# Transposing an attention step's probabilities: one DMA of 36 blocks in place of four of 2 to 16

## The chip, the cores and the metric

The kernel runs on one core of a Trainium2 chip, written directly against the engines: each of TensorE (PE), VectorE (DVE), ScalarE (ACT), GpSimd (POOL) and SyncE (SP) has a hand-written program, and semaphores order them. The metric is the time of one execution on the device in microseconds, the median of the runs of a kernel.

## The reference, cut to what matters

Two transformer blocks over 1024 tokens of width 256. The first attention and feed-forward are short here. What the change touches is the second attention: 32 heads of 64, 8 key/value heads (four query heads share one), rotary embedding, a causal mask, softmax, and the product with the values.

```python
x = x + _L0_attn_ref(_layernorm(x), Wq, Wk, Wv, Wo)
x = x + _L0_ffn_ref(_layernorm(x), w_gate_up, w_down)
x = x + _L1_attn_ref(_layernorm(x), wq, wk, wv, wo)
x = x + _L1_ffn_ref(_layernorm(x), w_fc, w_proj)

# _L1_attn_ref
xq = xq * cos + _rotate_half(xq) * sin
xk = xk * cos + _rotate_half(xk) * sin
scores = einsum('bqhd,bkhd->bhqk', xq, xk) * scale
scores = where(causal, scores, -inf)
probs = softmax(scores, axis=-1)
out = einsum('bhqk,bkhd->bqhd', probs, xv)
return out.reshape(...) @ wo
```

## The kernel before, in words

**Steps.** The second attention runs in 64 steps G (`STEPS`), eight for each of the 8 key/value groups. A step holds two heads and two query tiles of 128 rows, in two parts: with r = G % 4, part 0 has a query tile of 5 + r key blocks, part 1 one of 4 - r key blocks (`blocks`). With two heads that is 10, 12, 14 or 16 blocks of 128x128 in part 0 and 8, 6, 4 or 2 in part 1, 18 in every step.

**One step on its engines.** TensorE computes the scores of a part (L1330, and the mask by L1335). VectorE takes the row maxima (L964). ScalarE takes four exponentials (`exp_unit`, L658, two for each part) into `probs` in float32. The probabilities are then split in two float16 numbers: ScalarE casts them to the high part (`p_high`, L668), and GpSimd subtracts that from `probs` for the low part (`p_low`, L492). SP issues DMA transposes of the high and low parts (L371 and L377), since the product with the values needs the keys on the partitions. Three steps later (`PV_LAG = 3`) TensorE multiplies them with the values (`pv`): for each of the 18 blocks, high part times high values (L1353) and low values (L1357), then low part times high values (L1353). VectorE divides by the sum (L971, L973).

**Buffers.** `probs` and the two parts (`p16_hi`, `p16_lo`) have two buffers each, the transposed ones (`pT_hi`, `pT_lo`) three. So the exponentials of step G wait for the low parts of G-2, the high cast of part 0 of step G waits for the landing of both high transposes of G-2, the low part of G for both low ones of G-2, and the transposes of G for the `pv` of G-3.

**Order on each engine.** Each engine takes its instructions in order. ScalarE in step G: the high cast of part 1 of G-1, exponential 0, exponential 1, the high cast of part 0, exponentials 2 and 3, with copies for other work between them. TensorE's scores of a part wait for the exponentials of the same part of the step before (`exp_done`). GpSimd in step G: the rotary additions that fall due (L477, L480; eight of them in the first four steps of a group), low part 0, low part 1; in the sixth step of a group the low part of the next weights (`split_wkq_low`, L465) stands between the two, in the third the low part of the output weights (`split_wo_low`, L470), and the latter also in the last step of all. SP in step G: weight loads in two steps of a group, then the transposes high 0, high 1, low 0, low 1, each with a wait for its own part and a semaphore of its own.

**Other work.** `JOBS` lays the projections, transposes and output products of neighbouring groups between the scores and `pv` on TensorE. When the last `pv` is done, the output product, and after it the last feed-forward, follow.

**Names in the rows.** A program's tiles are shown with buffer numbers left out: `p_hi` and `p_lo` are the float16 parts, `pT_hi` and `pT_lo` their transposes.

Of the kernel before, what the change touches and what calls it, by code (L numbers as in the profile page):

```python
# [16 lines left out]
F32R = mybir.dt.float32r  # L17
F16 = mybir.dt.float16
# [5 lines left out]
P = 128  # L24
# [7 lines left out]
def transformer_program(nc, x_in, wq_a, wk_a, wv_a, wo_a, w_gate_up, w_down,  # L32
# [3 lines left out]
    KC = C // P  # L36
# [10 lines left out]
    def sb(name, kb, shape, dt):  # L47

        return nc.alloc_sbuf_tensor_at(name, [P] + shape, dt, offset=base + int(kb * 1024))
# [50 lines left out]
    v_lo = sb("v_lo", 88.25, [NT, NG * HEAD], F16)  # L100

    KQ = 5 * HEAD
    wkq_hi = sb("wkq_hi", 64.5, [KC, KQ], F32R)
    wkq_lo = sb("wkq_lo", 67, [KC, KQ], F32R)
    wo_nat = sb("wo_nat", 69.5, [2, C], F32)
    wo_hi = sb("wo_hi", 71.5, [2, C], F32R)
    wo_lo = sb("wo_lo", 73.5, [2, C], F32R)
# [6 lines left out]
    qT = [sb(f"qT{p}", 154 + 8 * p, [T], F32) for p in range(2)]  # L114

    probs = [sb(f"probs{b}", 42 + 9 * b, [18 * P], F32) for b in range(2)]
    p16_hi = [sb(f"p16_hi{b}", 186 + 9 * b, [18 * P], F16) for b in range(2)]
    p16_lo = [sb(f"p16_lo{b}", 190.5 + 9 * b, [18 * P], F16) for b in range(2)]
    pT_hi = [sb(f"pT_hi{b}", kb, [18, P], F16) for b, kb in enumerate((26, 30.5, 104.5))]
    pT_lo = [sb(f"pT_lo{b}", kb, [18, P], F16) for b, kb in enumerate((60, 128, 132.5))]  # L120
    o32 = [sb(f"o32{b}", kb, [4, HEAD], F32) for b, kb in enumerate((109.5, 110.5, 78, 79))]
    oT_hi = sb("oT_hi", 170, [2, T], F32R)
    oT_lo = sb("oT_lo", 178, [2, T], F32R)
# [38 lines left out]
    with ExitStack() as ctx:  # L162
        PS = ctx.enter_context(nc.psum_tensor("PS", [P, 8 * BANK], F32))

        def bank(b, n=1):
            return PS[:, b * BANK:(b + n) * BANK]
# [5 lines left out]
        def sem(name):  # L172
            return ctx.enter_context(nc.semaphore(name))
# [53 lines left out]

        scores_done, nmax_done, exp_done = sem("scores_done"), sem("nmax_done"), sem("exp_done")
        p_hi_done, p_lo_done = sem("p_hi_done"), sem("p_lo_done")
        pT_hi_landed = [[sem(f"pT_hi_landed{part}{b}") for b in range(3)] for part in range(2)]  # L230
        pT_lo_landed = [[sem(f"pT_lo_landed{part}{b}") for b in range(3)] for part in range(2)]
        pv_done, recip_done, norm_done = sem("pv_done"), sem("recip_done"), sem("norm_done")
        oT_done, oT_hi_done, oT_lo_done = sem("oT_done"), sem("oT_hi_done"), sem("oT_lo_done")
        wo_done = sem("wo_done")
# [26 lines left out]
        def of_step(G):  # L261
            g, n = G // 8, G % 8
            return g, n, n // 4, n % 4

        def blocks(G, part):
            r = G % 4
            return 4 - r if part else 5 + r
# [4 lines left out]
        def part_cols(G, part):  # L272
            n = 2 * blocks(G, 0)
            return slice(n, 18) if part else slice(0, n)
# [56 lines left out]
        def _(sp):  # L331
# [16 lines left out]
            def load_wkq(g):  # L348
                sp.dma_start(wkq_nat[:, :, 0:HEAD], rows(wk_b)[:, :, g * HEAD:(g + 1) * HEAD]).then_inc(wkq_landed, 16)
                sp.dma_start(wkq_nat[:, :, HEAD:KQ],  # L350
                             rows(wq_b)[:, :, 4 * g * HEAD:4 * (g + 1) * HEAD]).then_inc(wkq_landed, 16)
# [13 lines left out]
            load_wkq(1)  # L365
            sp.wait_ge(ternT_landed, 32)

            def transpose_hi(G, part):
                sp.wait_ge(p_hi_done, 2 * G + part + 1)
                sl = part_cols(G, part)  # L370
                sp.dma_start(pT_hi[G % 3][:, sl, :], p16_hi[G % 2][:, sl.start * P:sl.stop * P], transpose=True)\  # L371
                  .then_inc(pT_hi_landed[part][G % 3], 16)

            def transpose_lo(G, part):
                sp.wait_ge(p_lo_done, 2 * G + part + 1)
                sl = part_cols(G, part)
                sp.dma_start(pT_lo[G % 3][:, sl, :], p16_lo[G % 2][:, sl.start * P:sl.stop * P], transpose=True)\  # L377
                  .then_inc(pT_lo_landed[part][G % 3], 16)

            for G in range(STEPS):  # L380
                g, n, p, r = of_step(G)
                if n == 0 and g + 2 < NG:
                    sp.wait_ge(wkq_split, g + 2)
                    load_wkq(g + 2)
                if n == 4:
                    if g:
                        sp.wait_ge(wo_split, g)
                    load_wo(g)
                if G >= 3:
                    sp.wait_ge(pv_done, G - 2)  # L390
                transpose_hi(G, 0)
                transpose_hi(G, 1)
                transpose_lo(G, 0)
                transpose_lo(G, 1)

            for t in range(NT):
                sp.wait_ge(result_done, t + 1)
# [5 lines left out]
        def _(pool):  # L403
# [80 lines left out]
            def p_low(G, part):  # L484

                sl = part_cols(G, part)
                cols = slice(sl.start * P, sl.stop * P)
                pool.wait_ge(p_hi_done, 2 * G + part + 1)
                if G >= 2 and part == 0:
                    for landed in pT_lo_landed:  # L490
                        pool.wait_ge(landed[(G - 2) % 3], 16 * ((G - 2) // 3 + 1))
                nc.gpsimd.tensor_tensor(p16_lo[G % 2][:, cols], probs[G % 2][:, cols], p16_hi[G % 2][:, cols],  # L492
                                        ALU.subtract).then_inc(p_lo_done, 1)

            pool.wait_ge(gate_up_done, 2 * NF)
# [8 lines left out]
            for G in range(STEPS):  # L504
                g, n, p, r = of_step(G)
# [36 lines left out]
        def _(act):  # L542
# [118 lines left out]
            def p_high(G, part):  # L661
                sl = part_cols(G, part)
                cols = slice(sl.start * P, sl.stop * P)
                act.wait_ge(exp_done, 4 * G + 2 * part + 2)
                if G >= 2 and part == 0:
                    for landed in pT_hi_landed:
                        act.wait_ge(landed[(G - 2) % 3], 16 * ((G - 2) // 3 + 1))
                nc.scalar.copy(p16_hi[G % 2][:, cols], probs[G % 2][:, cols]).then_inc(p_hi_done, 1)  # L668

            split_wkq_high(0)  # L670
            for c in range(KC):
# [13 lines left out]
            for G in range(STEPS):  # L685
                g, n, p, r = of_step(G)
# [414 lines left out]
        def _(pe):  # L1101
# [238 lines left out]
            def pv(G, b):  # L1340

                g, buf, turn = G // 8, G % 3, G // 3 + 1
                o = bank(b)
                first = True
                for pT, landed in ((pT_hi, pT_hi_landed), (pT_lo, pT_lo_landed)):
                    for part in range(2):
                        pe.wait_ge(landed[part][buf], 16 * turn)
                        n, c = blocks(G, part), part_cols(G, part).start
                        for a in range(2):
                            u = (2 * part + a) * (HEAD + 1)  # L1350
                            for j in range(n):
                                p_block = pT[buf][:, c + a * n + j, :]
                                last = nc.tensor.matmul(o[:, u:u + HEAD + 1], p_block, v_hi[:, j, g, :], start=first,  # L1353
                                                        stop=False, skip_group_check=True)
                                first = False
                                if pT is pT_hi:
                                    nc.tensor.matmul(o[:, u:u + HEAD], p_block, v_lo[:, j, g * HEAD:(g + 1) * HEAD],  # L1357
                                                     start=False, stop=False, skip_group_check=True)
                last.then_inc(pv_done, 1)
# [153 lines left out]
```

## Time and profile before

| | us |
|---|---|
| median of 3 runs | 715.66 |
| lowest and highest | 710.64, 716.04 |
| the profiled execution | 710.78 |
| its span, first to last instruction | 709.0 |
| mean granted TensorE clock | 0.961 of full speed |

| engine | busy us | share |
|---|---|---|
| TensorE | 608.9 | 86% |
| GpSimd | 457.5 | 65% |
| ScalarE | 443.8 | 63% |
| VectorE | 436.8 | 62% |
| DMA queue of SP and its transposes | | 70.7% of 16 engines |

The page is one execution. Busy time is summed by engine; the slices show how it lies in time; the chain of what ended last and the waits show who was waited for. The attention in question runs from about 160 to 644 us. Most of its DMA traffic are the transposes: 36 blocks of 32 KB a step.

### The profile page before, as it was taken

Reading aid. Unit: us, or ns where it says so; the run is one execution under the profiler, and the core shown is the slowest. Engines: PE = TensorE matmul, PEld = TensorE weight load, DVE = VectorE, ACT = ScalarE, POOL = GpSimd, SP = SyncE. Lnnn points to the kernel's source line nnn. Section 1 sums busy time; section 2 is a strip of 40 time slices with the busy share of each in tenths; the row PEclk is TensorE's granted clock in tenths of the full one; section 3 lists DMA queues with packets and bytes.
Section 4 is the critical chain, followed back from the end, with each engine's and each line's share of the span. In section 5 each row is a group of like instructions: output and inputs, shape, how many; then the busy total and the mean of one; then the engine's idle time right before and its main releaser. Section 6 shows DMA issues by size and latency. Waiting matters only on the chain.

```text
span 709.0 us, 16178 instructions
## 1 busy us (share of the span) xinstructions
PE 608.9 (86%) x6750; PEld 478.5 (67%) x6750; DVE 436.8 (62%) x714; ACT 443.8 (63%) x599; POOL 457.5 (65%) x404
## 2 busy tenths in 40 slices
PE   4979988999879898987988889898798986975796
PEld 2767777986657776775776677677577664864375
DVE  5384377466657555755765675576576554555796
ACT  2223401148787677777867866877786788560695
POOL 6032155247979966977988698599689577562221
PEclk9998999999999999999999999999999999899699
DMA  9050003106999999999999999998999999991001
GB/s 296 1 178 1 1 0 67 31 0 120 153 173 171 176 169 159 177 160 182 164 168 179 165 176 160 176 178 158 186 160 159 173 159 176 182 147 35 1 23 37
DMA packets 321288, 91.76 MB, mean 129 GB/s; under 512 B 310080, under 2 KB 320320, under 8 KB 321216
## 3 DMA queue, kind: packets, MB, share of 16 engines
q1 hardware_dynamic: 320128, 89.69, 70.7%
q8 instruction: 53, 0.87, 0.5%
q10 hardware_dynamic: 1088, 1.05, 0.4%
q14 instruction: 19, 0.16, 0.1%
HBM read 13.11 MB, written 1.05 MB: 20 GB/s over the span
## 4 chain that ended last, share of the span: by engine, by line
PE 54%; DVE 14%; POOL 11%; ACT 10%; issue 5%; DMA 4%; SPq 1%; POOLq 0%; ACTq 0%; DVEq 0%
PE PS L1105 27%; PE PS L1330 13%; DVE small L964 7%; POOL p_lo L492 7%; PE PS L1353 5%; ACT probs L658 4%; PE PS L1270 3%; DMA pT_lo<-p_lo 3%; ACT p_hi L668 3%; PE PS L1357 2%; ACT oT_hi L639 2%; DVE oT_lo L979 1%; PE PS L1335 1%; POOL roped L480 1%; DMA pT_hi<-p_hi 1%
## 5 line engine op out<-in xcount | busy, mean ns | idle before, releaser
L492 POOL TENSOR_TENSOR p_lo<-probs,p_hi 128x1280 f16<-128x1280 f32 (+7 forms) x128 | 302.8, 2383 | 84.1 <-ACT p_hi L668 62.9
L658 ACT ACTIVATE probs<-PS,small 128x640 f32<-128x640 f32 (+7 forms) x256 | 183.6, 741 | 101.4 <-DVE small L964 101.4
L964 DVE TENSOR_REDUCE small<-PS 128x2 f32<-128x1280 f32 (+7 forms) x128 | 173.4, 1355 | 72.4 <-PE PS L1335 72.0
L1330 PE MATMUL PS<-kT,qT 64*128 64x512 f32 (+3 forms) x768 | 160.3, 522 | 23.7 <-ACT probs L658 22.5
L668 ACT CAST p_hi<-probs 128x1280 f16<-128x1280 f32 (+7 forms) x128 | 147.7, 1154 | 12.6 <-DMA pT_hi<-p_hi 9.2
L1330 PEld LDWEIGHTS PS<-kT,qT 64*128 64x128 f32 x768 | 65.0, 187 | 68.5 <-issue 57.1
L1353 PE MATMUL PS<-v_hi,pT_hi 128*128 128x65 f16 x1152 | 83.7, 199 | 4.1 <-DVE oT_lo L979 2.5
L1357 PE MATMUL PS<-v_lo,pT_hi 128*128 128x64 f16 x1152 | 83.2, 199 | 0.0
L1353 PEld LDWEIGHTS PS<-v_hi,pT_hi 128*128 128x128 f16 x1152 | 77.3, 102 | 8.0 <-DVE oT_lo L979 2.9
L1357 PEld LDWEIGHTS PS<-v_lo,pT_hi 128*128 128x128 f16 x1152 | 77.1, 101 | 0.4
L1105 PE MATMUL PS<-wo_hi,oT_hi 128*128 128x256 f32 x128 | 39.5, 308 | 17.1 <-DVE oT_lo L979 14.9
L979 DVE TENSOR_TENSOR oT_lo<-PS,oT_hi 128x512 fp32r<-128x512 f32 x32 | 22.1, 692 | 49.7 <-ACT oT_hi L639 49.7
L1335 PEld LDWEIGHTS PS<-mask_rows,pick_rows 64*128 64x128 bf16 x512 | 26.9, 96 | 33.9 <-issue 25.2
L1353 PE MATMUL PS<-v_hi,pT_lo 128*128 128x65 f16 x1152 | 46.6, 195 | 0.8 <-DMA pT_lo<-p_lo 0.8
L451 POOL TENSOR_TENSOR hT_lo<-h,hT_hi 128x512 fp32r<-128x512 f32 x16 | 23.6, 1479 | 36.5 <-DVE hT_hi L845 29.2
L480 POOL TENSOR_TENSOR roped<-t_cos,t_sin 128x256 f32<-128x256 f32 x64 | 47.1, 735 | 0.0
L1105 PE MATMUL PS<-wkq_hi,xnT_hi 128*128 128x320 f32 x128 | 44.8, 350 | 1.7 <-ACT qT L635 0.9
L440 POOL TENSOR_SCALAR moments<-moments 128x1 f32<-128x1 f32 x32 | 7.6, 236 | 58.4 <-DVE moments L756 57.8
L477 POOL TENSOR_TENSOR roped<-t_cos,t_sin 128x128 f32<-128x128 f32 x64 | 29.5, 461 | 19.8 <-DVE t_sin L924 19.8
L920 DVE TENSOR_TENSOR t_cos<-PS,cs 128x320 f32<-128x320 f32 x64 | 31.1, 486 | 17.0 <-POOL roped L480 9.2
L1353 PEld LDWEIGHTS PS<-v_hi,pT_lo 128*128 128x128 f16 x1152 | 40.4, 99 | 1.1 <-DMA pT_lo<-p_lo 1.1
L1270 PE MATMUL PS<-identf,roped 128*128 128x128 f32 x192 | 31.9, 298 | 9.8 <-DVE oT_lo L979 9.8
(184 smaller groups left out, 1248.2 us busy)
## 6 DMA issues: line engine op xcount, KB each, us to landing
wgu_nat<-L_ffn_w_gate_up SPq DMA_DIRECT2D x2, 1024.0 KB, 11.1
wkq_nat<-L_attn_wq SPq DMA_DIRECT2D x8, 256.0 KB, 3.5
pT_hi<-p_hi SPq DMA_TRANSPOSE x128, 4.0
pT_lo<-p_lo SPq DMA_TRANSPOSE x128, 4.1
wo_nat<-L_attn_wo SPq DMA_DIRECT2D x8, 256.0 KB, 3.4
x<-L_attn_x SPq DMA_DIRECT2D x4, 256.0 KB, 5.6
wdn_nat<-L_ffn_w_down SPq DMA_DIRECT2D x1, 1024.0 KB, 12.9
wfc_nat<-L_ffn_w_fc SPq DMA_DIRECT2D x1, 1024.0 KB, 5.8
```

Source lines behind the costliest of these rows:

```text
L480: nc.gpsimd.tensor_tensor(roped[:, t, P:3 * P], t_cos[b][:, 1:5, :].rearrange("p h d -> p (h d)"), t_sin[b][:, 1:5, :].rearrange("p h d -> ...
L492: nc.gpsimd.tensor_tensor(p16_lo[G % 2][:, cols], probs[G % 2][:, cols], p16_hi[G % 2][:, cols], ALU.subtract).then_inc(p_lo_done, 1)
L658: nc.scalar.activation(probs[G % 2][:, start:start + w], PS[:, src:src + w], ACT.Exp, bias=nmax[:, 4 * (G % 2) + u:4 * (G % 2) + u + 1]).t ...
L668: nc.scalar.copy(p16_hi[G % 2][:, cols], probs[G % 2][:, cols]).then_inc(p_hi_done, 1)
L920: nc.vector.tensor_tensor(t_cos[d][:], raw, cs[:, t, 0:HEAD].unsqueeze(1).broadcast_to(heads), ALU.mult)
L964: nc.vector.tensor_reduce(nmax[:, first:first + 2], both_heads(part)[:, :, 0:blocks(G, part) * P], AX.X, ALU.max, negate=True).then_inc(nm ...
L1105: last = nc.tensor.matmul(dst, lhsT, rhs, start=n == 0, stop=n == len(pairs) - 1)
L1270: last = nc.tensor.transpose(bank(b)[:, q * P:(q + 1) * P], roped[:, 4 * half + q, first:first + P], identf[:])
L1330: last = nc.tensor.matmul(dst[a], qT[p][rows_of[a], q_cols], kT[g % 2][rows_of[a], cols], start=True, stop=c0 + w < width, skip_group_chec ...
L1335: last = nc.tensor.matmul(dst[a][:, w - P:w], picked[rows_of[a], :], masked[rows_of[a], :], start=False, stop=m == 1, skip_group_check=True)
L1353: last = nc.tensor.matmul(o[:, u:u + HEAD + 1], p_block, v_hi[:, j, g, :], start=first, stop=False, skip_group_check=True)
L1357: nc.tensor.matmul(o[:, u:u + HEAD], p_block, v_lo[:, j, g * HEAD:(g + 1) * HEAD], start=False, stop=False, skip_group_check=True)
```

## The change

The high and low parts of a step share one buffer (`p16`, 2 x 18 blocks a partition), and so do their transposes (`pT`). SP issues one DMA transpose of all 36 blocks, when both low parts of the step are done, with one semaphore. The high cast and the low part of step G wait for the landing of this one transfer of step G-2. `pv` waits once, at its start. Two weight tiles (`wkq_hi`, `wkq_lo`) move to another place in memory to make room. The products and their order are as before.

```diff
-    wkq_hi = sb("wkq_hi", 64.5, [KC, KQ], F32R)
-    wkq_lo = sb("wkq_lo", 67, [KC, KQ], F32R)
+    wkq_hi = sb("wkq_hi", 104.5, [KC, KQ], F32R)
+    wkq_lo = sb("wkq_lo", 107, [KC, KQ], F32R)
...
-    p16_hi = [sb(f"p16_hi{b}", 186 + 9 * b, [18 * P], F16) for b in range(2)]
-    p16_lo = [sb(f"p16_lo{b}", 190.5 + 9 * b, [18 * P], F16) for b in range(2)]
-    pT_hi = [sb(f"pT_hi{b}", kb, [18, P], F16) for b, kb in enumerate((26, 30.5, 104.5))]
-    pT_lo = [sb(f"pT_lo{b}", kb, [18, P], F16) for b, kb in enumerate((60, 128, 132.5))]
+    p16 = [sb(f"p16_{b}", 186 + 9 * b, [2, 18 * P], F16) for b in range(2)]
+    pT = [sb(f"pT{b}", kb, [2, 18, P], F16) for b, kb in enumerate((26, 128, 60))]
...
-            def transpose_hi(G, part):
-                sp.wait_ge(p_hi_done, 2 * G + part + 1)
-                sl = part_cols(G, part)
-                sp.dma_start(pT_hi[G % 3][:, sl, :], p16_hi[G % 2][:, sl.start * P:sl.stop * P], transpose=True)\
-                  .then_inc(pT_hi_landed[part][G % 3], 16)
-
-            def transpose_lo(G, part):
-                sp.wait_ge(p_lo_done, 2 * G + part + 1)
-                sl = part_cols(G, part)
-                sp.dma_start(pT_lo[G % 3][:, sl, :], p16_lo[G % 2][:, sl.start * P:sl.stop * P], transpose=True)\
-                  .then_inc(pT_lo_landed[part][G % 3], 16)
+            def transpose_both(G):
+                sp.wait_ge(p_lo_done, 2 * G + 2)
+                sp.dma_start(pT[G % 3][:].rearrange("p s n q -> p (s n) q"),
+                             p16[G % 2][:].rearrange("p s n -> p (s n)"), transpose=True)\
+                  .then_inc(pT_landed[G % 3], 16)
...
-                transpose_hi(G, 0)
-                transpose_hi(G, 1)
-                transpose_lo(G, 0)
-                transpose_lo(G, 1)
+                transpose_both(G)
...
                 if G >= 2 and part == 0:
-                    for landed in pT_lo_landed:
-                        pool.wait_ge(landed[(G - 2) % 3], 16 * ((G - 2) // 3 + 1))
+                    pool.wait_ge(pT_landed[(G - 2) % 3], 16 * ((G - 2) // 3 + 1))
...
                 if G >= 2 and part == 0:
-                    for landed in pT_hi_landed:
-                        act.wait_ge(landed[(G - 2) % 3], 16 * ((G - 2) // 3 + 1))
-                nc.scalar.copy(p16_hi[G % 2][:, cols], probs[G % 2][:, cols]).then_inc(p_hi_done, 1)
+                    act.wait_ge(pT_landed[(G - 2) % 3], 16 * ((G - 2) // 3 + 1))
+                nc.scalar.copy(p16[G % 2][:, 0, cols], probs[G % 2][:, cols]).then_inc(p_hi_done, 1)
...
-                for pT, landed in ((pT_hi, pT_hi_landed), (pT_lo, pT_lo_landed)):
+                pe.wait_ge(pT_landed[buf], 16 * turn)
+                for s in range(2):
                     for part in range(2):
-                        pe.wait_ge(landed[part][buf], 16 * turn)
```

## Rows read from the trace of the kernel before

**Rows 1.** The page's slices, 40 of the span: share of DMA, in tenths

```profile
DMA  9050003106999999999999999998999999991001
```

**Rows 2.** Busy time by stretch: PE, PEld, DVE, ACT, POOL; clock; DMA share; GB/s

```profile
345.50:406.50 61.00, 55.38 (x730) 43.00 (x732) 38.30 (x58) 45.77 (x61) 49.31 (x36) 0.97 0.99 170
```

**Rows 3.** Waits from 200 to 620 us: total us, times, longest

```profile
POOL p_lo L492 <- DMA pT_lo<-p_lo: 21.0, 11, 3.5
...
PE PS L1330 <- ACT probs L658: 20.3, 10, 2.7
...
ACT p_hi L668 <- DMA pT_hi<-p_hi: 9.2, 8, 2.0
```

**Rows 4.** SP in order of time, steps 24 and 25: start, duration, line

```profile
347.00 3.07 SPq L371 DMA_TRANSPOSE pT_hi<-p_hi  x2
350.12 2.92 SPq L377 DMA_TRANSPOSE pT_lo<-p_lo  x2
353.14 3.21 SPq L371 DMA_TRANSPOSE pT_hi<-p_hi  x2
```

**Rows 5.** Tile pT_lo, step 24's two transposes, issued at 350.1 and 351.6 us

```profile
DMA to landing us min/median/max: 3.4/3.5/3.5
```

**Rows 6.** GpSimd in order of time: steps 0, 8, 24, 26, 28, 29, 32, 36, 56, 63

```profile
165.87 4.73 POOL L492 TENSOR_TENSOR p_lo<-probs,p_hi 128x1280 f16<-128x1280 f32 x2
...
218.85 4.72 POOL L492 TENSOR_TENSOR p_lo<-probs,p_hi 128x1280 f16<-128x1280 f32 x2
...
340.80 4.73 POOL L492 TENSOR_TENSOR p_lo<-probs,p_hi 128x1280 f16<-128x1280 f32 x2
...
360.90 1.15 POOL L492 TENSOR_TENSOR p_lo<-probs,p_hi 128x512 f16<-128x512 f32 x1
...
370.89 4.73 POOL L492 TENSOR_TENSOR p_lo<-probs,p_hi 128x1280 f16<-128x1280 f32 x2 [1.94 <-DMA pT_lo<-p_lo]
...
381.16 1.53 POOL L465 TENSOR_TENSOR wkq_lo<-wkq_nat,wkq_hi 128x640 fp32r<-128x640 f32 x1
...
401.75 4.73 POOL L492 TENSOR_TENSOR p_lo<-probs,p_hi 128x1280 f16<-128x1280 f32 x2
...
432.40 2.15 POOL L492 TENSOR_TENSOR p_lo<-probs,p_hi 128x1024 f16<-128x1024 f32 x1 [0.32 <-ACT p_hi L668]
...
583.22 2.13 POOL L492 TENSOR_TENSOR p_lo<-probs,p_hi 128x1024 f16<-128x1024 f32 x1 [0.85 <-ACT p_hi L668]
...
638.59 0.67 POOL L492 TENSOR_TENSOR p_lo<-probs,p_hi 128x256 f16<-128x256 f32 x1
```

**Rows 7.** To landing: all pT_hi; fcT, 16 blocks; pT_hi at 396.5 us, 16 blocks

```profile
DMA to landing us min/median/max: 2.3/4.0/6.1
...
fcT<-tern SPq DMA_TRANSPOSE x1, 4.5
...
DMA to landing us min/median/max: 5.6/5.6/5.6
```

**Rows 8.** ScalarE's high cast by shape, 330 to 390 us: busy, mean ns

```profile
L668 ACT CAST p_hi<-probs 128x2048 f16<-128x2048 f32 x2 | 3.8, 1898 | 0.1
...
L668 ACT CAST p_hi<-probs 128x1280 f16<-128x1280 f32 x2 | 2.5, 1259 | 0.1
```

**Rows 9.** The chain that ended last, at the end of the attention: start, us, what

```profile
633.26 0.07 issue
...
637.43 5.83 DMA pT_lo<-p_lo
643.26 0.05 issue
643.31 0.74 PE PS L1353 x18
```

**Rows 10.** TensorE in order of time: first and last matmul of 36, step 63

```profile
641.68 0.20 PE L1353 MATMUL PS<-v_hi,pT_hi 128*128 128x65 f16 x1
...
642.75 0.19 PE L1357 MATMUL PS<-v_lo,pT_hi 128*128 128x64 f16 x1
```

More of the change, by code:

```diff
@@ L229, in transformer_program @@
         p_hi_done, p_lo_done = sem("p_hi_done"), sem("p_lo_done")
-        pT_hi_landed = [[sem(f"pT_hi_landed{part}{b}") for b in range(3)] for part in range(2)]
-        pT_lo_landed = [[sem(f"pT_lo_landed{part}{b}") for b in range(3)] for part in range(2)]
+        pT_landed = [sem(f"pT_landed{b}") for b in range(3)]
         pv_done, recip_done, norm_done = sem("pv_done"), sem("recip_done"), sem("norm_done")
@@ L489, in p_low @@
                 if G >= 2 and part == 0:
-                    for landed in pT_lo_landed:
-                        pool.wait_ge(landed[(G - 2) % 3], 16 * ((G - 2) // 3 + 1))
-                nc.gpsimd.tensor_tensor(p16_lo[G % 2][:, cols], probs[G % 2][:, cols], p16_hi[G % 2][:, cols],
+                    pool.wait_ge(pT_landed[(G - 2) % 3], 16 * ((G - 2) // 3 + 1))
+                nc.gpsimd.tensor_tensor(p16[G % 2][:, 1, cols], probs[G % 2][:, cols], p16[G % 2][:, 0, cols],
                                         ALU.subtract).then_inc(p_lo_done, 1)
@@ L1351, in pv @@
                             for j in range(n):
-                                p_block = pT[buf][:, c + a * n + j, :]
+                                p_block = pT[buf][:, s, c + a * n + j, :]
                                 last = nc.tensor.matmul(o[:, u:u + HEAD + 1], p_block, v_hi[:, j, g, :], start=first,
@@ L1355, in pv @@
                                 first = False
-                                if pT is pT_hi:
+                                if s == 0:
                                     nc.tensor.matmul(o[:, u:u + HEAD], p_block, v_lo[:, j, g * HEAD:(g + 1) * HEAD],
```

## The prediction

> **What bounds the kernel now.** I read the page's slices first, for the DMA line, then the busy times of one group of eight attention steps, then who waited for whom in the attention, then the transposes and the low parts in order of time, and last the chain at the end of the attention. The DMA line stands at nine tenths through the whole attention, the slices of about 160 to 640 us, and low outside it [rows 1]. In the group from 345.5 to 406.5 us TensorE works 55.4 of 61.0 us, GpSimd 49.3, ScalarE 45.8, and the DMA engines' share is 0.99 [rows 2]. So there are two near-bounds, TensorE and the stream of transposes, and no engine has 20% to give without the other being felt. Landings hold GpSimd up for 21.0 us and ScalarE for 9.2 us; TensorE waits 20.3 us for exponentials [rows 3]. That is the whole of what an easier DMA could win back directly: some 30 us of waits off TensorE, of which TensorE saw at most 20.
>
> The order of the transposes matters. Step 24's low parts are complete at 340.80 + 4.73 = 345.5 us [rows 6]. Its four transposes are issued from 347.00 to 353.04 us, back to back, and the next step's begin at 353.14 us [rows 4]. The second low one is issued at 351.6 and lands 3.5 us later, at 355.1 us [rows 5]: 9.6 us after the low parts. The high ones went ahead of it. In other steps the high ones go out before the low parts exist, which is what four separate waits allow.
>
> **What goes.** Three issues in four, at about 1.5 us of SP's time each (3.07 and 2.92 us for two) [rows 4]. SP has no other work in the attention but a few loads in a group, and nobody waits for SP as such, so by itself this is worth nothing on the path. Three of four waits before TensorE's probabilities x values go too: nothing, as PV of a step comes three steps later. The moved buffers for the wkq split change no instruction: nothing.
>
> **What one transfer of 36 blocks costs.** The trace has none; I bound it. A transpose of 2 blocks lands in 2.3 us, the least of all; the 16 blocks of the ternary weights took 4.5 us with an idle stream [rows 7]. That is (4.5 - 2.3)/14 = 0.157 us a block, and 2.3 + 34 x 0.157 = 7.6 us for 36. Transfers are disturbed now and then: 16 blocks issued at 396.5 us took 5.6 us, 1.1 us over the quiet one, and the longest took 6.1 [rows 7]. A transfer of over 7 us meets such a disturbance often. I take half of the 1.1 us, 0.6 us: 8.2 us from issue to landing. The ends are 7.6 us (never disturbed) and 9.0 us (always, and a little of the step before still in the queue). The lower end is not the floor of doubt: if blocks of one transfer move faster than those of four, it could be near 6.6 us, and I keep that as a rival.
>
> The Trainium skill speaks for the change here: "DMA: Bandwidth & Descriptors", section "Anatomy of one DMA", puts a fixed cost of about 2.0 us on each DMA, and its "Rules for kernel authors" say to coalesce many small transfers. By that rule alone three fixed costs would go from each step. The rows agree on the size of a first cost (2.3 us for the smallest), but they show the four issues overlapping, so that most of it isn't paid four times.
>
> **What moves: the new loop.** Everything of a step now leaves after its last low part, and lands together. ScalarE's high cast of step G waits for the landing of step G-2, the whole of it, where it waited for the high half only. So a loop closes over two steps:
> - last low part of G-2 to landing: 8.2 us
> - high cast of part 0 of G: 1.26 to 1.90 us by the step, mean 1.58 us [rows 8]
> - the two low parts of G on GpSimd: 4.73 us together [rows 6]
> - three hand-overs, under 0.1 us each (0.05 and 0.07 us in the chain) [rows 9]: 0.2 us
>
> This is 14.7 us for two steps, and 58.8 us for eight. Once in eight steps the wkq low part (1.53 us) stands between two low parts of an odd step, and the wo one between those of an even step [rows 6]: each parity's loop takes one, so 58.8 + 1.5 = 60.3 us for eight steps.
>
> Before, the first eight steps took 223.6 - 170.6 = 53.0 us from one last low part to the other, and the next 48 took 585.4 - 223.6 = 361.8 us, 60.3 us for eight [rows 6]. So the loop is as long as the period that the kernel has, with no slack. In the first group it costs 60.3 - 53.0 = 7.3 us. That group ran ahead while the stream was still empty.
>
> The loop also stands in a worse place than the old wait. ScalarE runs in order: behind the waiting cast stand the exponentials of part 1, the other cast, and the next step's exponentials; TensorE's scores of the next step wait for these. Take step 28. Step 26's last low part ends at 360.90 + 1.15 = 362.1 us [rows 6], so it would land at 362.1 + 8.2 = 370.3 us; before, step 28's low part waited for a landing until 370.9 us [rows 6], but the cast was done ahead of it, since the high parts had landed. Now the cast alone ends at 370.3 + 1.26 = 371.6 us, and two exponentials and a cast come after it. Now the halves of a group: four steps took 375.6 - 345.5 = 30.1, 406.5 - 375.6 = 30.9 and 434.6 - 406.5 = 28.0 us [rows 6], against 60.3/2 = 30.2 us for the loop. Where the loop is longer than a half (2.2 us in the third) it sets the pace, and where TensorE's work is longer the loop's lead is lost in part. I charge 0.6 us a group for this, between 0 and the 2.2 us: 7 x 0.6 = 4 us.
>
> **What lies bare at the end.** Step 63's second low part ends at 638.59 + 0.67 = 639.3 us [rows 6]. Before, the large low transpose left at 637.43 and took 5.83 us, while the 36 matmuls of the high half (641.68 to 642.9, 1.3 us) ran under it; 0.74 us of low ones followed, to 644.05 us [rows 9, 10]. After: issue at 639.3, landing at 647.5, then 1.3 + 0.7 = 2.0 us of matmuls, end at 649.5 us. The rest of the kernel hangs on this: +5 us (4.8 with an undisturbed 7.6 us). This term hardly depends on the loop.
>
> **Sum.** First group +7, the six others at 60.3 us +0, alternation +4, end +5: +16 us. The profiled execution took 710.8 us (a span of 709.0 and 1.8 around it), so 727 us. The median of the three runs was 715.7, 0.7% above it, since two of them lay at 716; a median may fall anywhere between, and I say 728 us.
>
> **Rivals.** (1) Slack hides the loop: the groups keep their pace, because landings were late before too (9.6 us after the low parts in step 24), the second group gives back the first one's loss, and only the end is paid. 711 + 5 = 716 us, within 1%. For it: before, GpSimd waited for landings only 11 times. Against: ScalarE now waits for them too, ahead of the exponentials. Chance 0.22. (2) Faster: the stream is the real bound, and one transfer uses it better. It decides if 36 blocks land in under about 6.8 us: the loop is then 4 x 13.3 + 1.5 = 55 us, and TensorE's own 55.4 us of work in a group of 61 leaves perhaps 2.5 us a group to gain; 6 x 2.5 = 15 us less, 5 us more for the end: 701 us. For it: the share of 0.99 [rows 2] and the skill's rule above. Against: 0.157 us a block held between 2 and 16 blocks. Chance 0.12. (3) Each transfer is disturbed: 9.0 us, the loop 61.9 us for eight steps and 1.5 more from alternation: 7 x 63.4 - 414.8 = +29, and +6 at the end: 746 us. Chance 0.1. (4) TensorE's waits grow so long that its clock is granted at half more often: it was granted 0.97 in the group shown [rows 2]; at 0.93 another 4% of some 420 us of attention would be 17 us on top, 745 us. Chance 0.06. My own case: 0.5.
>
> **Numbers.** Within 1% is about what a measurement of this kernel can tell from no change. Faster 0.12 is rival 2; same 0.22 is rival 1; slower 0.66 is the rest. My own case spans 719 us (quiet transfers: two steps take 14.1 us, so only the first group, some 3 us, and the end) to 738. The range that leaves out 2 in 10 runs from 712 to 745 us.
>
> **What would show it.** One transpose a step, landing 7.6 to 8.5 us after issue (wrong if under 7). ScalarE's cast waiting for DMA: from 9 us to 60 or more, in most steps. GpSimd waiting for the DMA: gone, its wait on the cast longer. The DMA share down from 0.99 to about 0.9. The last low part of step 8 at 228 to 231 us, with the first's at 170.6. The first probabilities x values matmul of step 63 some 8 us after the last low part. If ScalarE's waits for landings stay under 20 us, the loop isn't the cause of anything, and rival 1 or 2 holds.

## The result, and the profile after

| | before | after |
|---|---|---|
| median, us | 715.85 (4 runs) | 750.52 (4 runs) |
| lowest and highest | 710.64, 719.02 | 748.27, 753.32 |
| profiled execution, its span | 710.78, 709.0 | 748.27, 746.5 |
| ratio | | 1.050, 95% interval 1.045 to 1.054 |

The changed kernel is 5% slower. I had said slower, but by 12 us, and the measured time is 5.5 us above the upper end of my range.

The page after: the busy line of each engine, the DMA slices, and the chain that ended last, as shares of the span.

```profile
PE 614.5 (82%) x6750; PEld 482.0 (65%) x6750; DVE 436.3 (58%) x714; ACT 441.7 (59%) x599; POOL 457.8 (61%) x404
...
DMA  8040003008989879789878979979978977963001
...
PE 41%; DMA 20%; DVE 14%; ACT 13%; POOL 8%; issue 3%; ACTq 0%; POOLq 0%; SPq 0%; DVEq 0%
```

The engines do the same work in a longer span. The DMA slices have holes where before they stood at nine tenths [rows 1]. The chain has 20% of DMA in it, where the page before has 4%.

A stretch of 64.6 us of the changed kernel, the length of one group of eight steps there, with columns as in [rows 2]:

```profile
350.30:414.90 64.60, 55.52 (x726) 43.92 (x726) 37.53 (x55) 46.22 (x61) 49.23 (x34) 0.95 0.85 157
```

Against [rows 2], TensorE's and GpSimd's work is the same; 3.6 us more are idle, and the DMA share fell from 0.99 to 0.85.

Waits of the changed kernel from 200 to 640 us: us in total, times, longest.

```profile
POOL p L479 <- ACT p L654: 95.9, 41, 4.5
...
ACT p L654 <- DMA pT<-p: 63.8, 30, 5.0
...
PE PS L1316 <- ACT probs L645: 23.8, 12, 3.3
```

This answers [rows 3]. The high cast (now L654) waits for landings in 30 steps, 63.8 us (63.0 in the window of [rows 3]) against 9.2; GpSimd's low part no longer waits for DMA but for that cast. TensorE's wait for exponentials is no longer than before: 18.8 us in the window of [rows 3] against 20.3.

The changed kernel's transfers of 36 blocks, from issue to landing, over the whole kernel:

```profile
DMA to landing us min/median/max: 7.2/8.1/9.4
```

The changed kernel's GpSimd in order of time (start, duration), the low parts of steps 0 and 8:

```profile
163.74 4.72 POOL L479 TENSOR_TENSOR p<-probs,p 128x1280 f16<-128x1280 f32 x2
...
222.63 4.86 POOL L479 TENSOR_TENSOR p<-probs,p 128x1280 f16<-128x1280 f32 x2 [0.24 <-ACT p L654]
```

Step 0's last low part ends at 168.5 and step 8's at 227.5 us: 59.0 us for the first group, where [rows 6] has 53.0.

The changed kernel's ScalarE in order of time, in step 20:

```profile
313.70 1.48 ACT L645 ACTIVATE probs<-PS,small 128x640 f32<-128x640 f32 x2 [1.45 <-DVE small L950]
319.72 1.26 ACT L654 CAST p<-probs 128x1280 f16<-128x1280 f32 x1 [4.54 <-DMA pT<-p]
320.88 0.68 ACT L645 ACTIVATE probs<-PS,small 128x512 f32<-128x512 f32 x1
```

The cast stands 4.54 us for step 18's landing, and the exponentials of part 1 follow it.

The changed kernel's chain at the end of the attention (start, us, what), against [rows 9], and in the second fence the first product with the values of step 62 and of step 63, from TensorE in order of time:

```profile
671.19 7.31 DMA pT<-p
678.50 0.14 issue
678.63 0.19 PE PS L1339
...
679.89 0.57 PE PS L1339 x18
```

```profile
670.10 0.22 PE L1339 MATMUL PS<-v_hi,pT 128*128 128x65 f16 x1 [3.99 <-DMA pT<-p]
...
678.63 0.19 PE L1339 MATMUL PS<-v_hi,pT 128*128 128x65 f16 x1 [0.41 <-DMA pT<-p]
```

TensorE stood 3.99 us for step 62's landing. Ahead of step 63's products it stood only 0.41 us: until then it had the output products of step 62.

**Where the 37.5 us of the two spans went.** From the last low parts of both traces: step 0 ends 2.1 us earlier (168.5 against 170.6); the first group takes 6.0 us more (59.0 against 53.0); the six groups from step 8 to 56 take 385.5 us in place of 361.8, 64.25 a group against 60.3, 23.7 us more; steps 56 to 63 take 58.1 in place of 53.9, 4.2 us more; and from the last low part to the end of the kernel 75.4 in place of 69.7 us, 5.7 us more.

**The loop, member by member.** I worked this out from the start and end of every cast, low part and landing of steps 8 to 59 in each trace: the means, in us, of the way from the last low part of step G-2 to that of step G. In the kernel before, the landing is that of the low parts, and the cast starts ahead of it (a negative number).

| | to landing | landing to cast | cast | to low 0 | low 0 | between | low 1 | sum |
|---|---|---|---|---|---|---|---|---|
| before | 7.44 | -0.72 | 1.58 | 1.56 | 3.36 | 0.31 | 1.41 | 14.9 |
| after | 8.21 | 0.60 | 1.58 | 0.51 | 3.36 | 0.36 | 1.40 | 16.0 |
| my sum | 8.2 | 0.1 | 1.58 | 0.1 | 3.35 | 0.4 | 1.38 | 15.1 |

"My sum" is the prediction's loop. The landing and the work are as forecast. In the mean the cast starts 0.60 us after the landing, not 0.1, and the low part 0.51 us after the cast, not 0.1: 0.9 us for two steps, 3.6 us for eight. These are means over steps in which the landing comes last and steps in which something else does; in 34 of the 62 steps that have such a wait the cast starts within 0.3 us of the landing.

### The profile page after: what moved, and what is told of

Same layout as the page of the kernel before. It is cut to its first block, busy times and chain, and to the rows that moved or that the text cites. A ratio compares the mean times of both kernels' runs of the same rounds, so it can differ in the third digit from the quotient of the medians.

```text
span 746.5 us, 15986 instructions
## 1 busy us (share of the span) xinstructions
PE 614.5 (82%) x6750; PEld 482.0 (65%) x6750; DVE 436.3 (58%) x714; ACT 441.7 (59%) x599; POOL 457.8 (61%) x404
## 4 chain that ended last, share of the span: by engine, by line
PE 41%; DMA 20%; DVE 14%; ACT 13%; POOL 8%; issue 3%; ACTq 0%; POOLq 0%; SPq 0%; DVEq 0%
PE PS L1091 24%; DMA pT<-p 20%; PE PS L1316 8%; DVE small L950 7%; ACT probs L645 5%; ACT p L654 5%; POOL p L479 4%; PE PS L1339 3%; PE PS L1256 2%; ACT oT_hi L626 2%; PE PS L1343 2%; DVE oT_lo L965 1%; POOL moments L430 1%; DVE stats L740 1%; POOL hT_lo L439 1%
## 5 line engine op out<-in xcount | busy, mean ns | idle before, releaser
L479 POOL TENSOR_TENSOR p<-probs,p 128x1280 f16<-128x1280 f32 (+7 forms) x128 | 302.7, 2378 | 112.4 <-ACT p L654 111.4
L654 ACT CAST p<-probs 128x1280 f16<-128x1280 f32 (+7 forms) x128 | 147.6, 1153 | 76.5 <-DMA pT<-p 73.8
L1339 PE MATMUL PS<-v_hi,pT 128*128 128x65 f16 x2304 | 124.8, 199 | 19.1 <-DMA pT<-p 8.5
L1339 PEld LDWEIGHTS PS<-v_hi,pT 128*128 128x128 f16 x2304 | 118.5, 102 | 24.3 <-DVE oT_lo L965 9.8
L1343 PE MATMUL PS<-v_lo,pT 128*128 128x64 f16 x1152 | 85.2, 200 | 0.0
L1343 PEld LDWEIGHTS PS<-v_lo,pT 128*128 128x128 f16 x1152 | 79.0, 102 | 0.3
L1091 PE MATMUL PS<-wo_hi,oT_hi 128*128 128x256 f32 x128 | 41.1, 321 | 21.7 <-DVE oT_lo L965 18.1
L1091 PEld LDWEIGHTS PS<-wo_hi,oT_hi 128*128 128x128 f32 x128 | 26.6, 207 | 24.2 <-issue 19.5
L1091 PE MATMUL PS<-wkq_lo,xnT_hi 128*128 128x320 f32 x128 | 39.5, 309 | 0.0
L1091 PE MATMUL PS<-wkq_hi,xnT_lo 128*128 128x320 f32 x128 | 39.4, 308 | 0.0
```

Of the source, the lines that this page charges most:

```text
L479: nc.gpsimd.tensor_tensor(p16[G % 2][:, 1, cols], probs[G % 2][:, cols], p16[G % 2][:, 0, cols], ALU.subtract).then_inc(p_lo_done, 1)
L654: nc.scalar.copy(p16[G % 2][:, 0, cols], probs[G % 2][:, cols]).then_inc(p_hi_done, 1)
L1091: last = nc.tensor.matmul(dst, lhsT, rhs, start=n == 0, stop=n == len(pairs) - 1)
```

## The experiments

Times are medians; ratios are to the kernel before, measured on the same chip, with 95% intervals. Theory A was the loop: late single landing, high cast, low parts. Its rivals were that the late start costs by itself, that a single large transfer is bad, and that what costs is what queues behind the waiting cast.

### The late start alone

```diff
+                sp.wait_ge(p_lo_done, 2 * G + 2)
                 transpose_hi(G, 0)
```

> The kernel before, with one wait more: SP issues none of a step's four transposes before the last low part of the step is done. So it has the late start of the changed kernel without its single transfer and its single landing. Theory A (the loop: landing, high cast, low parts, with the landing at 8.2 us after the last low part): the high half lands some 5 us after the last low part and the cast isn't held; the low half lands at 8.5 to 9 us and holds GpSimd only, so the two-step loop has no cast in it and is 8.8 + 4.7 + 0.4 = 13.9 us against the 16.0 us measured after the change. Then this kernel is nearer to before: 716 to 730 us. Rival (the late start alone is the cause, whatever lands first): 745 us or more.

734.2 us, 1.028 (1.021 to 1.034). The waits of this kernel with four late transfers, from 200 to 600 us:

```profile
POOL p_lo L493 <- DMA pT_lo<-p_lo: 67.5, 31, 4.3
...
ACT p_hi L669 <- DMA pT_hi<-p_hi: 49.4, 31, 3.8
```

Between my two figures. Over half of the loss, 19 of 35 us, comes with four transfers too, when they start late. Here the low half lands 10 us after the last low part, later than the single transfer's 8.2, and holds GpSimd. I expected the high half after some 5 us and a cast that isn't held; it landed 6.65 us after the last low part in the mean, and the cast waited for it 31 times. So this kernel has waits of both kinds, and how much each costs is not told apart. That the single landing adds the rest by holding the cast still longer is an inference.

### Two transfers of 18 blocks

```diff
-            def transpose_both(G):
-                sp.wait_ge(p_lo_done, 2 * G + 2)
-                sp.dma_start(pT[G % 3][:].rearrange("p s n q -> p (s n) q"),
-                             p16[G % 2][:].rearrange("p s n -> p (s n)"), transpose=True)\
-                  .then_inc(pT_landed[G % 3], 16)
+            def transpose_half(G, s):
+                sp.wait_ge((p_hi_done, p_lo_done)[s], 2 * G + 2)
+                sp.dma_start(pT[G % 3][:, s], p16[G % 2][:, s], transpose=True)\
+                  .then_inc(pT_landed[s][G % 3], 16)
```

The cast waits for the first of the two, the low part for the second.

> The changed kernel's shared buffers, but two transposes of 18 blocks a step with a semaphore each: the high one when both high parts are done, the low one after the last low part. The cast waits for the high one of two steps ago, GpSimd for the low one. Theory A: the low one lands about 2.3 + 16 x 0.157 = 4.8 us after the last low part, the loop is open again, and the time is that of before or a little less, 708 to 720 us. Rival (few large transfers are bad in themselves, or the shared buffer is): it stays above 730 us.

712.3 us, 0.998 (0.994 to 1.002): no difference to before. So the shared buffer and halving the number of transfers together cost and give nothing; what the change loses comes with the last merge, that of high and low. The waits of this kernel for landings, from 200 to 600 us:

```profile
ACT p L654 <- DMA pT<-p: 2.3, 3, 1.2
POOL p L479 <- DMA pT<-p: 1.5, 1, 1.5
```

### Two transfers, the cast waiting for both

The edit is against the kernel of two transfers.

```diff
                 if G >= 2 and part == 0:
+                    act.wait_ge(pT_landed[1][(G - 2) % 3], 16 * ((G - 2) // 3 + 1))
                     act.wait_ge(pT_landed[0][(G - 2) % 3], 16 * ((G - 2) // 3 + 1))
```

> As the kernel with two transposes of 18 blocks, but the high cast waits for both landings of two steps ago, as in the changed kernel. So the cast hangs on the low landing again, but that lands at about 4.8 us, not 8.2 us. Theory A: the loop is 4.8 + 0.6 + 1.6 + 0.5 + 5.1 = 12.6 us for two steps, under the period of 15, so the joint wait costs little: within 1.5% of the kernel with separate waits. Rival (what costs is that the cast waits for the low half at all, with the exponentials queued behind it): 735 us or more.

719.9 us, 1.008 (1.005 to 1.011), and 1% over the kernel with separate waits, as theory A had it. The cast hangs on the low landing as in the changed kernel: 19 casts start within 0.3 us of it, against 34 there. The landing comes 5.5 us after the last low part (mean over steps 8 to 55) in place of 8.2, and 31 of the 35 us are gone. What the joint wait costs shows in the first group, 57.8 us against 51.6 by the profiles; the six groups behind it take no longer.

### Four blocks less in the transfer

```diff
-                sp.dma_start(pT[G % 3][:].rearrange("p s n q -> p (s n) q"),
-                             p16[G % 2][:].rearrange("p s n -> p (s n)"), transpose=True)\
+                sp.dma_start(pT[G % 3][:].rearrange("p s n q -> p (s n) q")[:, 0:32, :],
+                             p16[G % 2][:].rearrange("p s n -> p (s n)")[:, 0:32 * P], transpose=True)\
```

> The changed kernel with 32 blocks in the transfer in place of 36: the last four low blocks of each step are left out of it (zeros stand in their place), everything else is as it was. The transfer lands about 0.63 us earlier. If the landing is a member of the loop that sets the time all through the attention, half of that is saved in each of 64 steps: 20 us, and 0.6 us at the end: 728 to 733 us. If the loop binds only in part of the steps, it is less: 738 to 745 us. If the landing doesn't bind: 750 us.

742.9 us, 1.038 (1.034 to 1.041). The landings of this kernel of 32 blocks over its whole run, and in the second fence its cast's waits from 200 to 640 us:

```profile
DMA to landing us min/median/max: 6.6/7.4/8.7
```

```profile
ACT p L656 <- DMA pT<-p: 50.3, 26, 4.1
```

The mean landing came 0.58 us earlier (7.63 after 8.21). If the loop set every step, that would be 64 x 0.58/2 = 18.6 us; the medians give 7.6 us, 41% of it, and the intervals of the two ratios leave some 5 to 12 us. So the landing is the last to arrive in some of the steps and not in all, and in the others something else is, by the waits the chain of TensorE, VectorE and ScalarE. How many steps these are is known only roughly: 41% by this run, and 30 of some 55 casts by the waits of the changed kernel. The joint kernel gained 31 us for a landing 2.7 us earlier, where 86 would come if every step were bound; but there the loop falls below the old period before all of that is used, so it is no second measure of the share.

### Three buffers: the loop opened

```diff
-    p16 = [sb(f"p16_{b}", 186 + 9 * b, [2, 18 * P], F16) for b in range(2)]
+    p16 = [sb(f"p16_{b}", kb, [2, 18 * P], F16) for b, kb in enumerate((186, 195, 96.5))]
...
-                if G >= 2 and part == 0:
-                    act.wait_ge(pT_landed[(G - 2) % 3], 16 * ((G - 2) // 3 + 1))
+                if G >= 3 and part == 0:
+                    act.wait_ge(pT_landed[G % 3], 16 * (G // 3))
```

and the same on GpSimd; the two weight tiles move once more to make room. The last feed-forward reads other values there, in products of the same number and size.

> The changed kernel, one transfer of 36 blocks after the last low part, with three buffers of the float16 parts in place of two, so that the high cast and the low part of step G wait for the landing of step G-3. The third buffer lies over the transposed ternary weights, and the last feed-forward reads that buffer in their place: its products are the same in number and size, their values are not the reference's. Theory A (the loop over two steps, and what queues behind the waiting cast, is the whole loss but for the end): landings are 7 us less pressing, ScalarE no longer waits for them, groups of 59 to 61 us, and 5 us for the end remain: 714 to 724 us. Rival (the single late transfer costs by itself, by the stream or by TensorE's wait for it three steps later): over 735 us.

723.8 us, 1.011 (1.007 to 1.015). The waits of the kernel with three buffers from 200 to 640 us, and in the second fence its landings:

```profile
ACT probs L647 <- DVE small L954: 110.5, 78, 4.1
POOL p L481 <- ACT p L658: 85.1, 35, 4.5
```

```profile
DMA to landing us min/median/max: 7.3/8.7/9.5
```

The transfer is as late and as long as in the changed kernel, no cast waits for it, and 27 of 35 us are back. This is the run that shows the wait of the cast and the low part for the landing of two steps earlier as the cause of most of the loss. A third buffer could also have freed waits that have nothing to do with the merge, and a kernel of two or four transfers with three buffers was not tried. But the kernel of two transfers has only 3.8 us of waits for landings in 400 us, so there is little of this kind to free.

What is left shows in three places, by the profiled executions (726.3 us for this kernel, 2.5 over its median, against 710.8 before, 5 under its median, so these figures are rather high). The first group still takes 57.9 us (59.0 with the loop, 53.0 before). In it TensorE waits for the landing itself, from 168 to 228 us:

```profile
PE PS L1343 <- DMA pT<-p: 3.7, 2, 2.9
```

The six groups behind it take 61.3 us each, 1.0 more than before and 3.0 less than in the changed kernel. And the last of TensorE's products with the values ends 9.3 us after the last low part, as in the changed kernel, against 4.8 before.

### The cast behind the exponentials, in three kernels

```diff
                 exp_unit(G, 1)
-                p_high(G, 0)
                 exp_unit(G, 2)
                 side(G, 1)
                 side(G, 2)
                 exp_unit(G, 3)
+                p_high(G, 0)
```

In the changed kernel:

> The changed kernel with one change of order on ScalarE: the high cast of part 0, which waits for the landing, stands behind the two exponentials of part 1 instead of ahead of them. The loop over two steps is as long as before or longer; only what stood behind the waiting cast is freed. If the 4 us that a group of eight steps takes over the loop that I predicted come from exponentials blocked behind the cast (and TensorE's scores behind them): groups of 61 us and 728 to 738 us. If they come from the loop itself, whose members (late cast, rotary additions ahead of the low part) each add their own delay: no gain or a loss, 748 to 765 us.

732.9 us, 1.026 (1.018 to 1.033). By my expectation that would have shown that exponentials queued behind the waiting cast make up half of the loss. The control says otherwise. With two transfers, where the cast hardly waits:

> The kernel with two transposes of 18 blocks a step and separate waits, with the high cast of part 0 behind the exponentials of part 1. In that kernel the cast hardly waits for a landing. If what the changed order gave there (18 us) was the release of exponentials blocked behind a waiting cast, it gives nothing here, or loses, since the cast and with it the low part come some 1.5 us later in each step: 710 to 722 us. If the order is better in itself: 698 to 705 us, which would beat both kernels.

696.6 us, 0.973 (0.969 to 0.977): 15.7 us less than the same kernel in the old order, where the changed kernel gained 17.7. The order is better in itself. What the single transfer costs is the same with either order, as far as this can tell: 750.5 - 712.3 = 38.2 and 732.9 - 696.6 = 36.3 us. So the two exponentials queued behind the waiting cast, which is all that the order frees, have no price that shows; the intervals leave room for some 8 us either way. What stands behind the cast in both orders (the second cast, the next step's exponentials) is not tested by this. This kernel beats both that this document began with. Its waits from 200 to 600 us have none on a DMA, the first being

```profile
ACT probs L645 <- DVE small L950: 93.0, 82, 2.9
```

In the kernel before:

> The kernel before, four transposes a step, with the high cast of part 0 behind the exponentials of part 1 and nothing else changed. If this order is what gave 16 to 18 us to both the changed kernel and the one with two transposes, it gives as much here: 697 to 702 us. If it needs the transposes of 18 blocks, because the stream of four is at its limit (share 0.99): 708 to 716 us.

708.7 us, 0.991 (0.988 to 0.995): 7 us, at the edge of what I expected if the stream of four is the limit. It still waits for landings, from 200 to 600 us:

```profile
POOL p_lo L492 <- DMA pT_lo<-p_lo: 14.7, 9, 3.2
```

So over half of the order's gain needs two transfers in place of four. Merging transfers is worth 12 us here, but only with the new order on ScalarE; that the stream of four is then the limit is suggested by these waits and not shown by an edit of its own.

### Three buffers and the later cast

The edits of the last two sections together.

> The kernel with one transfer of 36 blocks and three buffers of the float16 parts (the last feed-forward again reads the third buffer in place of the ternary weights, so values are not the reference's), with the high cast of part 0 behind the exponentials of part 1. It stands beside the kernel with two transfers and the same order (696.6 us): both have their loop open. If the loop is all that makes the single transfer slow between start and end, it is that kernel plus 5 us at the end and 3 to 5 us in the first group: 703 to 709 us. If a single transfer of 36 blocks is worse for the stream or for TensorE in the middle too: over 715 us.

712.5 us, 0.997 (0.995 to 0.999), between my two figures. Opening the loop gave 20.3 us here (732.9 to 712.5), of the 36.3 that the single transfer costs in this order; in the kernel of two transfers with this order no landing is waited for, so a third buffer would free nothing there. 16 us over that kernel remain. By the profiles, 13.9 us apart, 3.8 of them lie in the first group (58.9 against 55.1), 6.4 in the six groups between (59.2 against 58.1 us each), 2.6 in steps 56 to 63 and 2.7 behind them, less 1.6 ahead of step 0. So a single late transfer costs about 1 us a group in the middle even with the loop open. The waits from 200 to 600 us point to where:

```profile
PE PS L1343 <- DMA pT<-p: 8.3, 10, 2.9
```

TensorE itself waits for a landing ten times, 8.3 us in all, and in the kernel of two transfers never in this window. The prediction put this wait at nothing, as the products come three steps later. No edit took it away, so that it is the cause is not shown.

### The end in two transfers

```diff
+                if G == STEPS - 1:
+                    for s, done in enumerate((p_hi_done, p_lo_done)):
+                        sp.wait_ge(done, 2 * G + 2)
+                        sp.dma_start(pT[G % 3][:, s], p16[G % 2][:, s], transpose=True).then_inc(last_landed[s], 16)
```

TensorE waits for the high half and for the low half of step 63 by themselves.

> The changed kernel with the last step's transfer in two, high parts as soon as they are done, low parts after the last low part, and TensorE waiting for each. My account of the end: the low half lands 4.8 us after the last low part in place of 7.4, and the 1.3 us of matmuls on the high half go under it, so 3.5 to 4.5 us less than the changed kernel: 746 to 747 us. Rival (the 5.7 us of the end lie elsewhere): within 1 us of the changed kernel.

750.5 us, 1.050 (1.046 to 1.053): nothing. The low half of step 63 landed 5.1 us after the last low part, as expected, but the chain of this kernel with the split end ran elsewhere:

```profile
663.51 7.81 DMA pT<-p
...
673.58 0.99 PE PS L1348 x18
...
676.97 4.78 PE PS L1097 x24
...
682.86 0.57 PE PS L1348 x18
```

Step 62's transfer, its products and then its output products on TensorE stand ahead of step 63's products and are just as late. They ran at a low clock in this execution besides: the 24 output products took 4.8 us, and 3.1 us in the changed kernel's profile. The window from 675 to 683 us, columns as in [rows 2] (the clock is the third figure from the end), first of this kernel and then of the changed kernel:

```profile
675.00:683.00 8.00, 6.51 (x73) 6.09 (x72) 0.94 (x2) 0.59 (x1) 0.00 (x0) 0.64 0.22 41
```

```profile
675.00:683.00 8.00, 5.53 (x82) 5.06 (x82) 1.06 (x3) 0.58 (x1) 0.00 (x0) 1.00 0.43 80
```

The chain of the changed kernel does run as I forecast, through step 63's landing. But TensorE's work of step 62 is a second path, only 0.41 us shorter, as two transfers are late there and not one. So the split had 0.4 us to win even at the full clock, and not the 3.5 to 4.5 that I expected.

### The rotary addition behind the low part

```diff
-                for slot in range(3):
-                    name = job(G, slot)
+                names = [job(G, slot) for slot in range(3)]
+                for name in names[:2]:
                     if name[:1] == "r":
                         rope_add(NT * owner(G, name) + int(name[-1]))
                 p_low(G, 0)
+                if names[2][:1] == "r":
+                    rope_add(NT * owner(G, names[2]) + int(names[2][-1]))
```

In the changed kernel:

> The changed kernel, with the rotary addition of the third slot (there is one in the first and one in the third step of a group) behind the low part of part 0 on GpSimd, no longer ahead of it. In the changed kernel the low part starts 0.9 us after the cast in these two steps, against 0.1 us where no addition stands ahead. If each such delay adds to the loop, since the loop has no slack, up to 1.6 us of 64.3 are saved in a group, 6 to 11 us in all: 739 to 745 us. If the loop has slack in those steps, or VectorE's products wait for the later addition: 748 to 755 us.

750.8 us, 1.050 (1.046 to 1.054): nothing. The low part comes sooner after the cast (0.37 us in the mean for 0.51) and the gap between the low parts is as much longer (0.63 for 0.36). In the fastest kernel:

> The kernel with two transposes of 18 blocks and the cast behind the exponentials of part 1 (696.6 us), with the rotary addition of the third slot behind the low part as well. There the loop through the landing is open, and the low part is no member of what sets the pace: 694 to 699 us. If low parts matter there too: 690 us.

711.1 us, 0.994 (0.992 to 0.996), so 14.5 us lost. VectorE's wait for the addition from 200 to 600 us, in the fastest kernel with the addition late and then with it in its old place:

```profile
DVE t_cos L908 <- POOL roped L468: 24.3, 18, 2.7
```

```profile
DVE t_cos L906 <- POOL roped L468: 9.5, 6, 1.6
```

VectorE's next rotary product needs the addition, and the row maxima stand behind it. This wait grew by 14.8 us, about what the kernel lost. So in this kernel the additions ahead of the low part are not a delay to be moved away; they belong to the other chain.

## Why the prediction was right or wrong

- **The landing** (8.2 us, 7.6 to 9.0): right. Median 8.1, from 7.2 to 9.4 us; 0.157 us a block held up to 36. (In "DMA: Bandwidth & Descriptors" of the Trainium skill, the section "Anatomy of one DMA" gives its fixed cost of 2.0 us for a DMA issued from GpSimd. The transposes here are issued from SP; the smallest took 2.3 us.)
- **No gain from the issues saved**: right. Halving them changed nothing in the old order.
- **The loop through the cast**: right in kind. The cast's wait for landings went from 9.2 to 63.0 us in the same window, and three buffers took 27 of 35 us away again.
- **TensorE's waits at nothing, as its products come three steps later**: wrong, though small. Over the whole kernel its products with the values wait 8.5 us for landings, against 0.8 before, most of it in the first group and at step 62.
- **First group +7**: it was +6.0 us, though not by the loop alone: it is +4.9 with the loop open.
- **The six others +0, and alternation +0.6 a group (4 us in all)**: here the prediction failed. They took 64.25 us, 3.95 more than before, 23.7 us in place of some 4. I compared two averages, the loop's 60.3 and the old period's 60.3 us, took the larger, and gave the meeting of the two chains 0.6 us. What the runs show in its place: with the loop opened by a third buffer the groups take 61.3 us, so 3.0 of the 3.95 us come from the coupling through the landing, though the loop by its own sum is no longer than the old period; the other 1.0 us comes with the late single transfer even so. And with 32 blocks, where the loop by its sum is 60.3 - 4 x 0.58 = 58.0 us, the groups take 63.5. My explanation is an inference from this: both chains run at once and meet in each step, at the cast and at the low part, and each meeting ends with the later of the two. With averages equal and steps uneven (landings from 7.2 to 9.4 us, steps with and without rotary work), the later is often above either average, and a loop without slack gives nothing back. How the 4 us part between the spread of the landings and uneven steps stays open.
- **Steps 56 to 63**: left out. I charged seven groups and forgot that an eighth runs to the end: 4.2 us.
- **The end +5**: 5.7 us, right in size, and the chain runs as forecast; the split of the last transfer showed that step 62's work is as late.
- **Exponentials queued behind the cast**: I named it as the reason for the alternation. With either order the single transfer costs 36 to 38 us, so the two exponentials of part 1 have no price that shows.
- **Rivals.** Slack that hides the loop: no. Faster by a better used stream: no, though 12 us of it were there for two transfers and another order on ScalarE. Disturbed transfers at 9.0 us: the price was near (746 us) by luck, as the mean landing was 8.2. TensorE's clock: 0.952 against 0.961 over the span, not a main cause, as TensorE's busy time grew by 5.6 us over the whole kernel and by 0.1 us in the groups of [rows 2] and its counterpart.
- **A slip in the sums**: the loop of 61.9 us in the third rival and the "some 3 us" of the quiet end leave out the 1.5 us a group of the weights' low parts, which the main sum has. With them the loop at 9.0 us is 63.5 us, and the first group at 7.6 us is 4.9 us longer, not 3.

## What to carry to other kernels

A merge of transfers is priced by when its last part is ready to leave and by who waited for the first, not by the starts that it saves. Here merging parts that are ready together (four transfers to two) cost nothing, and merging the high with the later low parts cost 38 us. When two chains of equal average length meet in every step, charge more than the larger average; here the groups came out 4 us in 60 above it. And run an order found while testing a theory on the kernel without the suspected cost too: here the same reorder gained as much there, which undid a conclusion and gave the best kernel, 696.6 us.

## What the runs showed of the hardware

- DMA transposes of blocks of 128x128 in float16, from SP, within on-chip memory: 2.3 us for 2 blocks, 4.5 to 6.7 us for 18 (median 4.9, in the kernel of two transfers in the old order), 6.6 to 8.7 for 32, 7.2 to 9.4 for 36.
- In the kernel before, the four issues of a step hold it about as long together (two of them some 3 us [rows 4]), but not evenly by size: one of 16 blocks, at 396.5 us, held it 1.3 us and the one of 2 blocks right behind it 2.3. In the changed kernel one issue of 36 blocks holds SP 5.3 to 6.3 us in one piece. SP's group of this kernel, by line (count, ns min/median/max, first and last start):

```profile
L367 SPq DMA_TRANSPOSE pT<-p x64: 5305/5441/6261, 168.5 to 671.2; - x64
```

What this costs a load that stands behind such an issue was not measured.
- Landings of the same 36 blocks lie in two clusters: of 64, 31 from 7.2 to 7.7 us, one at 7.9, and 32 from 8.2 to 9.4 us. The cause stays open.
